# Attention heads of 48 rows, two to a tile, in the two halves of TensorE's rows

## The reference, cut to what matters

```python
q, k, v = split(x @ W_q.T), split(x @ W_k.T), split(x @ W_v.T)   # 16 heads of 16
attn = softmax(scale * einsum('bnqd,bnkd->bnqk', q, k), axis=-1)
o = einsum('bnqk,bnkd->bnqd', attn, v)
```

## Time and profile before

| | us |
|---|---|
| median of 3 runs | 771.07 |
| profiled execution, span | 773.6 |
| TensorE matmul busy | 658.1 |
| VectorE busy | 431.5 |
| ScalarE busy | 381.9 |
| GpSimd busy | 55.0 |

### The profile page before, as it was taken

How to read it: one execution, slowest core, us unless ns; L and a number is a source line. 1 busy time by engine, 2 the same in 40 slices (tenths; PEclk the granted TensorE clock), 3 DMA queues, 4 the chain that set the end, 5 groups by cost and what they waited for, 6 DMA issues and landing times.

```text
span 773.6 us, 9912 instructions
## 1 busy us (share of the span) xinstructions
PE 658.1 (85%) x3426; PEld 436.7 (56%) x3426; DVE 431.5 (56%) x863; ACT 381.9 (49%) x729; POOL 55.0 (7%) x91
## 2 busy tenths in 40 slices
PE   2655289699989998799989998799899996999896
PEld 0411176554448876455468876354488765544585
DVE  0352078397536565588255575787165663984344
ACT  1333077426773446246863447067752554267710
POOL 4010111200000000200000000200000002000000
PEclk9755689859999999769999999689989999599999
DMA  8898521422000000502000001510000002220000
GB/s 264 292 296 285 171 87 54 95 57 44 2 1 1 1 28 28 113 13 43 2 2 1 1 28 33 118 33 11 0 0 0 14 14 62 61 44 2 1 1 28
DMA packets 34473, 44.97 MB, mean 58 GB/s; under 512 B 4736, under 2 KB 27392, under 8 KB 34304
## 3 DMA queue, kind: packets, MB, share of 16 engines
q1 hardware_dynamic: 30048, 31.87, 14.8%
q0 software_dynamic: 3872, 11.54, 5.6%
q10 hardware_dynamic: 512, 1.05, 0.4%
HBM read 28.45 MB, written 3.15 MB: 41 GB/s over the span
## 4 chain that ended last, share of the span: by engine, by line
PE 70%; DMA 11%; ACT 8%; DVE 6%; issue 2%; SPq 2%; ACTq 0%
PE psum L1071 31%; PE psum L1237 12%; PE psum L1257 8%; PE psum L1266 8%; DMA arena<-in_hyp_w 7%; DMA kst<-split 2%; PE psum L1057 2%; PE psum L1294 1%; DMA qst<-mrow_lo 1%; ACT arena L473 1%; ACT arena L613 1%; PE psum L1159 1%; PE psum L1090 1%; PE psum L1199 1%; PE psum L1144 1%
## 5 line engine op out<-in xcount | busy, mean ns | idle before, releaser
L916 DVE TENSOR_REDUCE mx<-psum 128x1 f32<-128x512 f32 x256 | 160.9, 683 | 48.8 <-PE psum L1237 48.4
L613 ACT ACTIVATE arena<-psum 128x512 f32<-128x512 f32 x256 | 140.8, 601 | 67.0 <-PE psum L1257 66.0
L1237 PE MATMUL psum<-kst,qst 96*128 96x512 f32 x192 | 102.9, 623 | 22.5 <-DMA kst<-split 20.7
L1071 PE MATMUL psum<-act,ghw_hi 128*128 128x512 f32 (+1 forms) x288 | 93.6, 394 | 0.5 <-DVE act L728 0.2
L1237 PEld LDWEIGHTS psum<-kst,qst 96*128 96x128 f32 x192 | 49.7, 261 | 72.4 <-DVE mx L916 41.1
L1257 PE MATMUL psum<-qst,kst 98*128 98x512 f32 x192 | 83.4, 454 | 3.6 <-DMA qst<-mrow_lo 1.8
L1071 PE MATMUL psum<-upw_hi,kst 128*128 128x512 f32 x256 | 72.2, 404 | 0.0
L1057 PE MATMUL psum<-arena,hblk 128*32 128x256 f32 x256 | 31.0, 579 | 44.3 <-DMA arena<-in_hyp_w 42.4
L1266 PE MATMUL psum<-arena,vals 128*17 128x512 f32 x512 | 67.4, 598 | 1.3 <-ACT arena L613 1.0
L1071 PEld LDWEIGHTS psum<-act,ghw_hi 128*128 128x128 f32 x288 | 56.7, 208 | 11.3 <-DVE act L728 1.7
L639 ACT ACTIVATE arena<-psum 128x512 f32<-128x512 f32 x32 | 19.2, 599 | 85.0 <-PE psum L1071 85.0
(11 more groups left out here) (162 smaller groups left out, 1025.2 us busy)
## 6 DMA issues: line engine op xcount, KB each, us to landing
arena<-in_hyp_w SPq DMA_DIRECT2D x32, 512.0 KB, 5.2
kst<-split POOLq DMA_DIRECT2D x44, 128.0 KB, 4.0
qst<-split SPq DMA_DIRECT2D x72, 64.0 KB, 3.4
arena<-in_x SPq DMA_DIRECT2D x4, 512.0 KB, 3.5
arena<-in_up_w POOLq DMA_DIRECT2D x8, 256.0 KB, 7.7
arena<-in_gh_w POOLq DMA_DIRECT2D x8, 256.0 KB, 3.8
out_x<-arena SPq DMA_DIRECT2D x8, 256.0 KB, 2.1
act<-split SPq DMA_DIRECT2D x24, 64.0 KB, 2.3
```

Of the source, the lines that this page charges most:

```text
L613: s.activation(probs[:, kb % 2, i, :], bank[3 + n % RING], ACT.Exp).then_inc(a_p, 1)
L916: v.reduce_max(mx[:, g % 2, col:col + 1], bank[u % RING], AX.X).then_inc(d_max, 1)
L1071: ins = pe.matmul(dst, lhs(a, c), rhs(z, c), start=start and n == 0, stop=stop and n == len(terms) - 1, skip_group_check=skip)
L1237: pe.matmul(bank[u % RING], qst[g % 3][0:KROWS, i, P * t:P * t + P], keys_of(g)[0:KROWS, i // 2, :], start=True, stop=True).then_inc(e_max, 1)
```

## The change

A head's stack becomes 3 blocks of 16 rows, 48 in all, and 50 with the two rows of the maximum. Even heads stand at rows 0 to 49 of a tile, odd heads at rows 64 to 113. Query tiles become 2 wide as key tiles are, and there are three of each. No zeros are needed; the ones are set once; `act` is no longer a query tile, and the projections' input `inp` moves to query tiles 1 and 2. The memsets of `act` and of the ones in each batch go, with their semaphores.

A max tile and a score are now matmuls with 48 and 50 rows that start at row 0 or 64 (64x128 tiles of the array). For groups 1 to 3 the max tiles alternate between an odd and an even head, the odd one first; group 0 keeps the old order, the two even heads and then the two odd.

GpSimd issues six DMAs of 64 KB per group instead of three of 128 KB (four instead of two in group 0), the low keys of group 0 go in two halves, and the maximum's rows go in four DMAs per group instead of two. Keys have semaphores for even and odd heads.

```diff
-KROWS = 3 * 32
+PAIR = 64
+KROWS = 3 * DH
 SROWS = KROWS + 2
...
-        kst = [sb(f"kst{i}", [P, G // 2, L], F32R) for i in range(3)]
-        qst = [sb(f"qst{i}", [P, G, L], F32R) for i in range(2)] + [act_both]
-        inp = kst[0:2]
+        kst = [sb(f"kst{i}", [P, G // 2, L], F32R) for i in range(RINGS)]
+        qst = [sb(f"qst{i}", [P, G // 2, L], F32R) for i in range(RINGS)]
+        inp = qst[1:3]
...
+        def rows_of(tile, i, rows):
+            at = PAIR * (i % 2)
+            return tile[at:at + rows, i // 2, :]
+        def max_order(g):
+            if g == 0:
+                return [(i, t) for i in (0, 2, 1, 3) for t in range(T)]
+            return [(2 * (r // 8) + 1 - r % 2, r // 2 % T) for r in range(G * T)]
...
-                if g == 2:
-                    sp.wait_ge(act_zero, b + 1)
                 for e in range(2):
                     for k, part in enumerate((0, 1, 0)):
-                        dst = qst[g % 3][32 * k + DH * e:32 * k + DH * e + DH, e::2, :]
+                        dst = qst[g % 3][PAIR * e + DH * k:PAIR * e + DH * k + DH, :, :]
...
+                    for e in range(2):
+                        row = PAIR * e + KROWS + k
+                        dst = qst[g % 3][row:row + 1, :, :].rearrange("p i (t n) -> p (i t) n", t=T)
+                        sp.dma_start(dst.bitcast(F32), mrow[k][2 * T * e:2 * T * e + 2 * T, :].bitcast(F32)
+                                     ).then_inc(rows_in, 16)
...
-                for k, part in enumerate((0, 0, 1) if g > 0 else (0, 0)):
+                for e in range(2):
+                    for k, part in enumerate((0, 0, 1) if g > 0 else (0, 0)):
+                        dst = kst[g % 3][PAIR * e + DH * k:PAIR * e + DH * k + DH, :, :]
...
-                for i in range(2):
-                    pool.memset(kst[i][KROWS:SROWS, :, :].bitcast(F32), 1.0).then_inc(keys_ones, 1)
...
-                    pe.matmul(bank[u % RING], qst[g % 3][0:KROWS, i, P * t:P * t + P],
-                              keys_of(g)[0:KROWS, i // 2, :], start=True, stop=True).then_inc(e_max, 1)
+                    pe.matmul(bank[u % RING], rows_of(qst[g % 3], i, KROWS)[:, P * t:P * t + P],
+                              rows_of(kst[g % 3], i, KROWS), start=True, stop=True).then_inc(e_max, 1)
...
-                    pe.matmul(bank[3 + k % RING], keys_of(g)[0:SROWS, i // 2, P * kb:P * kb + P],
-                              qst[g % 3][0:SROWS, i, :], start=True, stop=True).then_inc(e_score, 1)
+                    pe.matmul(bank[3 + k % RING], rows_of(kst[g % 3], i, SROWS)[:, P * kb:P * kb + P],
+                              rows_of(qst[g % 3], i, SROWS), start=True, stop=True).then_inc(e_score, 1)
```

More of the change, by code:

```diff
@@ L44 @@
 HYP_SCALE = 0.1
-KROWS = 3 * 32
+PAIR = 64
+KROWS = 3 * DH
 SROWS = KROWS + 2
+RINGS = 3
 V_W, V_BIAS, V_LINB, V_BD, V_BU = 0, 2, 4, 6, 7
@@ L64 @@
 TURN_HEADS = 12
-HEAD_ORDER = (0, 2, 1, 3)
 RING = 3
@@ L130, in build, with max_column @@
         hh_s = [[split[:, 2 * p + n, :] for n in range(2)] for p in range(2)]
-        def keys_of(g):
-            return kst[(g + 2) % 3]
+        def rows_of(tile, i, rows):
[5 more added lines that the diff above has]
+            return [(2 * (r // 8) + 1 - r % 2, r // 2 % T) for r in range(G * T)]
+        def max_column(i, t):
+            return (i % 2) * 2 * T + (i // 2) * T + t
         def cut(first_col, columns, **dims):
@@ L189, in build @@
         queries_in = [[sem(f"{e}_queries_in{i}") for i in range(3)] for e in ("even", "odd")]
-        keys_lo_in = sem("keys_lo_in")
-        keys_in = [sem(f"keys_in{i}") for i in range(3)]
+        keys_lo_in = [sem(f"{e}_keys_lo_in") for e in ("even", "odd")]
+        keys_in = [[sem(f"{e}_keys_in{i}") for i in range(3)] for e in ("even", "odd")]
         hblk_set = sem("hblk_set")
-        act_zero, keys_ones = sem("act_zero"), sem("keys_ones")
         rows_in, out_done = sem("rows_in"), sem("out_done")
@@ L325, in stack_q @@
                         src = split[32 * g + DH * e:32 * g + DH * e + DH, 4 * part:4 * part + 2, :]
-                        dst = qst[g % 3][32 * k + DH * e:32 * k + DH * e + DH, e::2, :]
+                        dst = qst[g % 3][PAIR * e + DH * k:PAIR * e + DH * k + DH, :, :]
                         sp.dma_start(dst.bitcast(F32), src.bitcast(F32)).then_inc(queries_in[e][g % 3], 16)
[L328 to L332, removed]
+                    if g == 0:
+                        if e == 0:
+                            sp.wait_ge(a_qk, b * 4 + 4)
+                            sp.wait_ge(d_qk, b * 4 + 4)
+                        sp.dma_start(kst[0][PAIR * e + 2 * DH:PAIR * e + 3 * DH, :, :].bitcast(F32),
+                                     split[DH * e:DH * e + DH, 6:8, :].bitcast(F32)).then_inc(keys_lo_in[e], 16)
             def maxima_rows(b, g):
@@ L363, in _ @@
             sp.wait_ge(out_done, 32 * B + 32)
-        POOL_READY = 6
+        POOL_READY = 3 + RINGS
         @block.gpsimd
@@ L376, in _ @@
                                    pattern=[[-1, P]], channel_multiplier=1).then_inc(pool_ready, 1)
-            for i in range(2):
-                pool.memset(qst[i][:, :, :].bitcast(F32), 0.0).then_inc(pool_ready, 1)
-            pool.memset(kst[2][:, :, :].bitcast(F32), 1.0).then_inc(pool_ready, 1)
+            for i in range(RINGS):
+                pool.memset(kst[i][:, :, :].bitcast(F32), 1.0).then_inc(pool_ready, 1)
             pool.memset(vals[:, :, :, :], 1.0).then_inc(pool_ready, 1)
@@ L384, in stack_k @@
                 if g >= 3:
-                    pool.wait_ge(keys_ones, b * 2 + 2)
                     pool.wait_ge(e_score, b * (NG * T * G) + T * G * (g - 2))
                     pool.sem_inc(keys_free, 1)
-                for k, part in enumerate((0, 0, 1) if g > 0 else (0, 0)):
-                    src = split[32 * g:32 * g + 32, 4 * part + 2:4 * part + 4, :]
-                    pool.dma_start(keys_of(g)[32 * k:32 * k + 32, :, :].bitcast(F32), src.bitcast(F32)
-                                   ).then_inc(keys_in[g % 3], 16)
+                for e in range(2):
+                    for k, part in enumerate((0, 0, 1) if g > 0 else (0, 0)):
+                        src = split[32 * g + DH * e:32 * g + DH * e + DH, 4 * part + 2:4 * part + 4, :]
+                        dst = kst[g % 3][PAIR * e + DH * k:PAIR * e + DH * k + DH, :, :]
+                        pool.dma_start(dst.bitcast(F32), src.bitcast(F32)).then_inc(keys_in[e][g % 3], 16)
             def load_stage(n):
@@ L410, in _ @@
             with pool.Fori(0, B) as b:
[L411 to L414, removed]
                 pool.wait_ge(a_qk, b * 4 + 4)
@@ L588, in maxima_out @@
                     if g >= 1:
-                        s.wait_ge(rows_in, b * (NG * 32) + 32 * g)
+                        s.wait_ge(rows_in, b * (NG * 64) + 64 * g)
                     s.activation(mrow[0][:, :], bank[7][0:G * T, 0:P], ACT.Copy, scale=-1.0).then_inc(a_mrow, 1)
@@ L914, in maxima @@
                         v.wait_ge(e_maxT, b * NG + g - 1)
-                    col = HEAD_ORDER[k // T] * T + k % T
+                    col = max_column(*max_order(g)[k])
                     v.reduce_max(mx[:, g % 2, col:col + 1], bank[u % RING], AX.X).then_inc(d_max, 1)
@@ L1220, in max_tile @@
                 def max_tile(u):
[L1222 to L1227, removed]
+                    g, k = u // (G * T), u % (G * T)
+                    order = max_order(g)
+                    i, t = order[k]
+                    e = i % 2
+                    if e not in [j % 2 for j, _ in order[:k]]:
+                        in_turn = 2 if g % 3 == 0 else 1
+                        pe.wait_ge(queries_in[e][g % 3], b * (3 * 16 * in_turn) + 3 * 16 * (g // 3 + 1))
                         if g == 0:
-                            pe.wait_ge(keys_in[0], b * (5 * 16) + 2 * 16)
-                            pe.wait_ge(keys_lo_in, b * 16 + 16)
+                            pe.wait_ge(keys_in[e][0], b * (5 * 16) + 2 * 16)
+                            pe.wait_ge(keys_lo_in[e], b * 16 + 16)
                         elif g == 3:
-                            pe.wait_ge(keys_in[0], b * (5 * 16) + 5 * 16)
+                            pe.wait_ge(keys_in[e][0], b * (5 * 16) + 5 * 16)
                         else:
-                            pe.wait_ge(keys_in[g], b * (3 * 16) + 3 * 16)
+                            pe.wait_ge(keys_in[e][g], b * (3 * 16) + 3 * 16)
                     if u >= RING:
                         pe.wait_ge(d_max, b * NU + u - RING + 1)
-                    pe.matmul(bank[u % RING], qst[g % 3][0:KROWS, i, P * t:P * t + P],
-                              keys_of(g)[0:KROWS, i // 2, :], start=True, stop=True).then_inc(e_max, 1)
+                    pe.matmul(bank[u % RING], rows_of(qst[g % 3], i, KROWS)[:, P * t:P * t + P],
+                              rows_of(kst[g % 3], i, KROWS), start=True, stop=True).then_inc(e_max, 1)
                 def turn_max(g):
```

6 lines of the change are left out of this document (1 added, 5 removed).

## The result

The change makes the kernel slower: 798.23 us (793.47 to 802.98, 4 runs) against 770.73 before, a ratio of 1.0356 (95% interval 1.0311 to 1.0401). Forecast were 767, and 755 to 790.

A forecast was written before the change was run, and what follows sets the result against it. TensorE was taken to bound the kernel, with VectorE binding group 0's max tiles. Per batch -0.6 + 1.2 - 1.1 + 1.5 - 2.6 + 0.6 = -1.0; four batches -4 gives 769.6, 767 for the runs, range 755 to 790.

The forecast's parts named there:

- rival 3: Start of group 3: first tile waits for the odd copies, issued last; about 1.4 us per batch, 772 to 773; chance 0.08.
- (a): Wait for the stacked keys before the first max tile: first even tiles need only half the keys, -0.6 us per batch.
- (b): Group 0's 16 max tiles: VectorE bounds them at 0.60 us per tile, which stays; change 0.
- this stall: In front of group 0's first odd tile, whose copies have no slack: listed as a sign of being wrong, without a price.
- (c): Maximum's rows ahead of the first score: four issues on SyncE instead of two, +1.2 us per batch.
- (d): First seven scores with their max tiles, up to the first weigh: VectorE becomes the bound, 5.9 us, -1.1 per batch.
- one slow block at 1.5: Behind the first weigh: the clock is still low, so one block takes 4.2 us instead of 2.65, +1.5 per batch.
- (e): Blocks with max tiles: max tile and score overlap, a plain block takes 2.65 us instead of 3.06; -2.6 per batch.
- Switches: Places where 64-row tiles meet full-array ones, some ten per batch: changing between them costs +0.6 us per batch.
- the last group's rows: Maximum's rows of groups 1 to 3: a stall of 0 to 0.6 us was called possible, counted as 0.
- Rival 2: Max tiles and scores: tiles in different halves do not overlap; +6 us, 777; chance 0.12.
- Rival 4: Whole attention from the first weigh on: the clock never rises, 68 us in all, 839; chance 0.18, wholly or in part.

The follow-up runs named there:

- e1: Kernel after, with group 3 given key and query tiles of its own, so its copies wait for no score: 775.28 us, ratio 1.0062.
- e10: Kernel before, with only the maximum's rows in four DMAs per group instead of two: 776.44 us, ratio 1.0072.
- e3: e1 with TensorE's idle time ahead of and among the first max tiles filled with unused full-height matmuls: 840.40 us, ratio 1.0943.
- e5: Kernel before, with only the change's finer copies of keys and maximum's rows, group 0's low keys still in one DMA: 793.38 us, ratio 1.0307.
- e4: Kernel before, with TensorE's idle time ahead of and among the first max tiles filled with unused full-height matmuls: 769.69 us, ratio 0.9993.
- e9: Kernel before, with only the keys in six DMAs of 16 rows instead of three of 32 (group 0 four, not two): 786.08 us, ratio 1.0193.
- e11: e1 with each maximum row sent to both halves in one DMA, and idle matmuls before the first score and behind the first six: 764.66 us, ratio 0.9912.

## Why the prediction was wrong

- **The step that failed** is group 3's copies. They were no term of the sum: rival 3 had the mechanism, with a chance of 0.08 and 1.4 us per batch. It had 7.3 from the first issue to the last landing and TensorE there after 5.8. Measured in the second batch are 8.7 (355.92 to 364.63) and 5.4, a wait of 3.5; that block is 3.5 longer than before, and the one behind it, at the low clock, 0.8. The sum had both 0.3 to 0.5 shorter than before. Without the wait the kernel is some 22 us faster (e1). I carried the issue and landing times of before over, although half-height key copies now ran beside the queries'. The 22 issues for 11 on GpSimd's queue were named under (a), and no time was put on them.
- **Keys (a)**: -0.7 for -0.6, right. But only the even tiles profited: the low keys of the odd heads were issued at 322.50, 4.1 behind the even ones with three queries between, landed 5.6 later, and the first odd tile started at 328.32 after a gap of 1.03. **(b)**, costed at 0, is +1.1 for that. The prediction had this stall among its signs of being wrong, with no price. It is the same error: what is issued last had no slack.
- **Rows (c)**: +0.9 here for +1.2, and 5.3 us in four batches by itself (e10) for 4.8. Right.
- **First scores (d)**: -1.6 for -1.1, right in kind, and the clock was at 0.50 at the first weigh, as said. The sum counted ten max tiles behind the first score; the trace of before has nine, since the tenth ran ahead of it, and one of VectorE's steps of 0.60 is the difference. The term behind it, one slow block at 1.5, was mis-sized: three blocks in three of the batches and two in the first, +3.2 in all in the second batch. A slow block took 3.84, 4.14, and 4.88 with turn_max; 4.2 was forecast.
- **Blocks (e)**: 2.69 and 2.78 for 2.65. The mechanism was right. Of eight blocks four gave 1.0 us together, the others were slow or waited. In e1, where nothing waits, the seven blocks from the third weigh on (346.42 to 366.55) take 20.1, as forecast (20.2). The forecast took 3.71 for both blocks with turn_max before; the second took 2.94 (367.83 to 370.77), so less was to be had from it.
- **Switches**: 1.1 in the blocks without max tiles against 0.6 forecast for all; 0.2 of it is in a block in which TensorE waits 0.62 for the last group's rows, which were costed at 0. e3 gives 0.2 for one switch at the high clock, 0.3 at the low one.
- **Rival 2** (no overlap) is out. **Rival 4** (the clock never rises) is out as a whole; in part it happened, four slow blocks of fifteen.

By experiment the books are: copies +24 (e5), tiles with all that follows from them +5 (798.2 - 793.4). The tiles alone were not tried with the copies of before, so +5 is a difference and not a measurement of its own: two heads' rows of a key block no longer lie next to each other, so the keys' copies belong to the layout.

## What to carry to other kernels

When a layout is made finer, price its copies first: count issues per queue, and take the time of the *last* one to the first instruction that wants it. A consumer order that alternates between two halves wants both at once, and so wants the last. Before believing in idle time, look which buffer's release starts the copy; a tile of its own for group 3 was worth some 22 us here (e1), the overlap 1.0 per batch between the weighs of the kernel after.

## What the runs showed of the hardware

- A 64-row tile in the free half of TensorE's rows cost no time of its own: starts 358.06 and 358.06, 0.50 and 0.49 long, and the next pair starts at 358.39, 0.33 later, as a single tile's successor behind a weigh does before (349.27, 349.61).
- Alternating tiles of 48 and 128 rows costs 0.2 (high clock) to 0.3 us (low) per switch (e3); alternating 96 and 128 rows costs nothing (0.23 apart, e4).
- With the keys in copies of 16 rows instead of 32, the DMA engines were busy half as long again over the same bytes (129 against 197 GB/s at full share, queries' copies included). Six of SyncE's issues take 3.77 with no copy of GpSimd's being issued (before, 325.64), 5.22 beside three (before, 350.04), and 5.81 and 6.38 beside six (e9, 350.61; after, 355.92, one issue of 2.58).
- The granted clock fell to 0.50 under gapless tiles of alternating height (e3, 336.6) and, in one batch of four, among half-height scores (e11, 372), and stayed at 1.00 in the kernel before over the same scores at full height.
